# Where the expert-value block stands within a quarter, and the order of the third quarter

## The reference, cut to what matters

```
x = x + 0.5 * ffn(layernorm(x))
x = x + attn(layernorm(x))          # linear attention over states, 16 heads of 8
x = x + 0.5 * ffn(layernorm(x))
```

```
q, k   = x Wq, x Wk                       # 16 heads, 64 wide
w, sel = top2(x Ws);  mix = sigmoid(w) at sel, else 0
v[h]   = sum_e mix[h, e] * (x Wv[e])      # the "values"
attn   = softmax(q k / 8) v               # "scores", "turn", "product"
mask   = top2 of (x Wd) per head
res    = sum_h sum_e mask[h, e] * (attn[h] Wo[e])   # "expand" and "output"
```

## Time and profile before

| | us |
|---|---|
| median of 3 runs | 2470.3 |
| lowest and highest of the 3 | 2469.51 and 2485.37 |
| the profiled execution, its own time | 2470.45 |
| its span, first to last instruction | 2468.7 |
| TensorE busy in it | 2348.8 (95%) |
| ScalarE busy | 2083.6 (84%) |
| VectorE busy | 1960.9 (79%) |
| GpSimd busy | 1136.0 (46%) |
| DMA, mean rate over the span | 157 GB/s |

### The profile page before, as it was taken

The page is one execution under the profiler, slowest core; times in us unless marked ns, Lnnn a source line. Parts: engine busy times, 40 slices in busy tenths (PEclk is TensorE's granted clock), DMA queues, the critical chain, the costliest instruction groups (busy, mean ns, idle before and its releaser), DMA issues.

```text
span 2468.7 us, 119467 instructions
## 1 busy us (share of the span) xinstructions
PE 2348.8 (95%) x49920; PEld 2165.5 (88%) x49920; DVE 1960.9 (79%) x3498; ACT 2083.6 (84%) x6373; POOL 1136.0 (46%) x1126
## 2 busy tenths in 40 slices
PE   3999999999999999999999999999999999999997
PEld 3888898989889898888989889899898989989897
DVE  4887877878888788888888788787887887888874
ACT  3988888888888888888888889888888888889896
POOL 3454544535445355354454444553453544544431
PEclk9999999999999999999999999999999999999999
DMA  4565555655656655566656556566665655565564
GB/s 129 160 162 149 150 158 150 160 152 158 170 150 163 163 157 155 156 162 165 158 157 165 149 156 167 165 163 155 169 159 154 170 157 157 157 167 155 160 173 107
DMA packets 519381, 388.09 MB, mean 157 GB/s; under 512 B 214080, under 2 KB 436160, under 8 KB 510656
## 3 DMA queue, kind: packets, MB, share of 16 engines
q1 hardware_dynamic: 518416, 379.60, 57.5%
q10 hardware_dynamic: 432, 0.85, 0.1%
HBM read 191.64 MB, written 188.74 MB: 154 GB/s over the span
## 4 chain that ended last, share of the span: by engine, by line
PE 82%; DVE 8%; ACT 5%; issue 4%; POOL 1%; DMA 1%; SPq 0%; ACTq 0%; DVEq 0%; POOLq 0%
PE psT L453 18%; PE psS L408 15%; PE psT L470 7%; PE psS L496 6%; PE psT L421 6%; PE psT L472 6%; PE psT L471 6%; PE psT L496 5%; PE psT L465 5%; ACT PB L767 4%; PE psT L435 3%; DVE NMAX L647 1%; DVE QK L706 1%; PE psT L502 1%; DVE ST L729 1%
## 5 line engine op out<-in xcount | busy, mean ns | idle before, releaser
L767 ACT ACTIVATE PB<-psS,NMAX 128x256 f32<-128x256 f32 x2048 | 943.5, 488 | 71.3 <-DVE NMAX L647 68.0
L453 PE MATMUL psT<-V,PT 128*64 128x64 f32 x16384 | 550.0, 224 | 42.9 <-issue 42.2
L453 PEld LDWEIGHTS psT<-V,PT 128*64 128x64 f32 x16384 | 508.7, 138 | 74.0 <-issue 48.8
L706 DVE TENSOR_TENSOR QK<-psT,QK 128x512 fp32r<-128x512 f32 x512 | 341.8, 688 | 205.0 <-ACT QK L776 202.6
L408 PE MATMUL psS<-QK 64*128 64x256 f32 x6144 | 480.4, 291 | 0.2
L767 ACT ACTIVATION_READ_ACCUMULATOR PB<-psS,NMAX 128x1 f32 x2048 | 453.3, 221 | 0.0
L408 PEld LDWEIGHTS psS<-QK 64*128 64x128 f32 x6144 | 404.5, 186 | 32.1 <-issue 29.5
L647 DVE TENSOR_REDUCE NMAX<-psS 128x2 f32<-128x512 f32 x512 | 328.6, 683 | 85.7 <-PE psS L408 84.8
L776 ACT ACTIVATE QK<-psT 128x512 fp32r<-128x512 f32 x512 | 298.1, 621 | 112.5 <-PE psT L472 98.1
L875 POOL TENSOR_TENSOR BT<-MT,diagv 128x1024 f32<-128x1024 f32 x128 | 305.9, 2390 | 136.1 <-DMA MT<-MIXd 136.1
L856 ACT ACTIVATE PT<-psS 128x512 f32<-128x512 f32 x512 | 280.1, 604 | 52.2 <-PE psS L496 48.4
(11 more groups left out here) (119 smaller groups left out, 4589.3 us busy)
## 6 DMA issues: line engine op xcount, KB each, us to landing
Vd<-VM SPq DMA_DIRECT2D x128, 512.0 KB, 3.9
V<-Vd SPq DMA_DIRECT2D x128, 512.0 KB, 5.2
AOd<-AO SPq DMA_DIRECT2D x256, 256.0 KB, 3.8
PJd<-PJ SPq DMA_DIRECT2D x64, 512.0 KB, 2.8
PR<-PJd SPq DMA_DIRECT2D x64, 512.0 KB, 4.0
MIXd<-MIX SPq DMA_DIRECT2D x64, 128.0 KB, 1.7
MT<-MIXd SPq DMA_DIRECT2D x64, 128.0 KB, 4.4
MASKd<-MASKR SPq DMA_DIRECT2D x64, 128.0 KB, 4.0
```

The source lines that it names most:

```text
L453: last = eng.matmul(M[64 * u:64 * u + 64, (t * NT + it) * DH:(t * NT + it + 1) * DH], PT[:, t, jt, cols], V[:, pm % 2, 4 * r + t, jt, :], ...
L706: eng.tensor_tensor(QK[:, 1, ab], bank("qk", m).rearrange("p (k t) -> p k t", k=2), QK[:, 0, ab].bitcast(F32), ALU.subtract).then_inc(free ...
L767: eng.activation(PB[:, ab, j, it, :], psS[:, ab, j, it, :], ACT.Exp, bias=NMAX[:, ab, j, it:it + 1], accum_out=SUM[:, p % 2, it, 4 * r + t ...
```

## The change

The two halves of `values` leave the front of the third and fourth quarters (r = 2 and 3, behind `scores`) and go to the ends of the second and third (r = 1 and 2), right ahead of `turn`. Their places in the ring move with them. On ScalarE `copy_values` stays in r = 2 and r = 3, but now comes ahead of `exponentials(n, 0)`. In the third quarter the q and k projections of the next quarter come right behind `expand`, ahead of `xturn`, `attn_x` and `attn_gram`, on TensorE, in the ring, on VectorE (`QK` ahead of `XT`) and on ScalarE (`rounded` ahead of the copies of `XT`, `AXT` and `GRAM`). No instruction's work is changed; GpSimd's and SyncE's programs are the same.

```diff
--- before.py
+++ after.py
@@ -163,23 +163,19 @@
 
             p, r = divmod(n, 4)
             items = []
-            if r == 2 and runs(p + 1):
-                items += [("values", p + 1, 0, a) for a in range(2)]
-            if r == 3 and runs(p + 1):
-                items += [("values", p + 1, 1, a) for a in range(2)]
             if r == 1 and runs(p - 2):
                 items += [("output", p - 2, i) for i in range(2)]
             if works(n - 1):
                 items.append(("product", n - 1))
             if r == 2 and runs(p - 1):
                 items += [("expand", p - 1, b) for b in range(2)]
+            if works(n + 1):
+                items += [("qk", 2 * n + 2), ("qk", 2 * n + 3)]
             if r == 2:
                 if runs(p + 3):
                     items.append(("xturn", p + 3))
                 if attends(p - 2):
                     items += [("attn_x", p - 2), ("attn_gram", p - 2)]
-            if works(n + 1):
-                items += [("qk", 2 * n + 2), ("qk", 2 * n + 3)]
             if r == 0:
                 if runs(p + 2):
                     items.append(("expert", p + 2, 0))
@@ -199,6 +195,8 @@
                     items.append(("attn_turn", p - 3))
                 if attends(p - 2):
                     items.append(("attn_keys", p - 2))
+            if r in (1, 2) and runs(p + 1):
+                items += [("values", p + 1, r - 1, a) for a in range(2)]
             if works(n):
                 items += [("turn", n, t) for t in (0, 1)]
             return items
@@ -507,10 +505,6 @@
                 if works(n):
                     scores(n, 0)
                     scores(n, 1)
-                if r == 2 and runs(p + 1):
-                    values(p + 1, 0)
-                if r == 3 and runs(p + 1):
-                    values(p + 1, 1)
                 if r == 1 and runs(p - 2):
                     output(p - 2)
                 if works(n - 1):
@@ -518,6 +512,9 @@
                 if r == 2 and runs(p - 1):
                     expand(p - 1, 0)
                     expand(p - 1, 1)
+                if works(n + 1):
+                    project(2 * n + 2)
+                    project(2 * n + 3)
                 if r == 2 and runs(p + 3):
                     q = p + 3
                     wait_vacant(eng, "xturn", q)
@@ -534,9 +531,6 @@
                     for t in range(NT):
                         last = eng.matmul(bank("attn_gram", q)[:, 0:C + 1], AXN[:, t, 0:C], AXN[:, t, :], start=t == 0, stop=t == NT - 1)
                     last.then_inc(full("attn_gram", q))
-                if works(n + 1):
-                    project(2 * n + 2)
-                    project(2 * n + 3)
                 if r in (0, 1) and runs(p + 2):
                     q = p + 2
                     wait_vacant(eng, "expert", q, r)
@@ -591,6 +585,8 @@
                     for k in range(2):
                         last = eng.matmul(M[:, 2 * C + k:2 * C + k + 1], awkv[:, k * C:(k + 1) * C], GRAM[:, C:C + 1], start=True, stop=True)
                     last.then_inc(full("attn_keys", q))
+                if r in (1, 2) and runs(p + 1):
+                    values(p + 1, r - 1)
                 if works(n):
                     turn(n, 1)
                     turn(n, 0)
@@ -695,15 +691,15 @@
                         wait_full(eng, "output", p - 2, 0)
                         wait_full(eng, "output", p - 2, 1)
                         eng.tensor_copy(OT[:, :, 64 * b:64 * b + 64], bank("expand", p - 1, b).rearrange("p (e k) -> p e k", e=E)).then_inc(freed("expand", p - 1, b))
-                if r == 2 and runs(p + 3):
-                    dst = XT[:, (p + 3) % 4]
-                    eng.wait_ge(s_xhi, p + 4)
-                    eng.tensor_tensor(dst[:, 1, :], bank("xturn", p + 3)[:, 0:T], dst[:, 0, :].bitcast(F32), ALU.subtract).then_inc(freed("xturn", p + 3))
                 if works(n + 1):
                     for ab in range(2):
                         m = 2 * n + 2 + ab
                         eng.wait_ge(s_qhi, m + 1)
                         eng.tensor_tensor(QK[:, 1, ab], bank("qk", m).rearrange("p (k t) -> p k t", k=2), QK[:, 0, ab].bitcast(F32), ALU.subtract).then_inc(freed("qk", m))
+                if r == 2 and runs(p + 3):
+                    dst = XT[:, (p + 3) % 4]
+                    eng.wait_ge(s_xhi, p + 4)
+                    eng.tensor_tensor(dst[:, 1, :], bank("xturn", p + 3)[:, 0:T], dst[:, 0, :].bitcast(F32), ALU.subtract).then_inc(freed("xturn", p + 3))
                 if r == 2 and runs(q):
                     equal(1, GM[:, :, :], at + 7)
                 if r == 0 and runs(q):
@@ -790,14 +786,16 @@
                     if q >= 1:
                         eng.wait_ge(s_share, SHARES * (q - 1) + 3)
                     eng.activation(SG[:, :, :], MAXV[:, :, :].rearrange("p k (r g) -> p k g r", g=2)[:, :, 0, :], ACT.Exp, scale=-1.0).then_inc(s_sig)
-                if works(n):
-                    exponentials(n, 0)
                 if r == 2 and runs(p + 1):
                     copy_values(p + 1, 0)
                 if r == 3 and runs(p + 1):
                     copy_values(p + 1, 1)
                 if works(n):
+                    exponentials(n, 0)
+                if works(n):
                     exponentials(n, 1)
+                if works(n + 1):
+                    rounded(n)
                 if r == 2 and runs(p + 3):
                     q = p + 3
                     wait_full(eng, "xturn", q)
@@ -816,8 +814,6 @@
                         wait_full(eng, "attn_keys", attn_pass[nth[q] - 1])
                         wait_freed(eng, "attn_keys", attn_pass[nth[q] - 1])
                     eng.activation(GRAM[:, :], bank("attn_gram", q)[:, 0:C + 1], ACT.Copy).then_inc(freed("attn_gram", q))
-                if works(n + 1):
-                    rounded(n)
                 if r in (0, 1) and runs(p + 2):
                     q = p + 2
                     wait_full(eng, "expert", q, r)
```

## The result

The changed kernel takes **2607.07 us** (median of 4 runs, 2603.05 to 2609.01) against 2473.19 of the kernel before on the same chip: ratio 1.052, interval 1.0484 to 1.0556. The forecast was 2590, slower.

A forecast was written before the change was run, and what follows sets the result against it. The prediction took TensorE to bound the kernel, with almost no slack against ScalarE and VectorE. Waits of 5.6 us per pair of passes, times 32, gave 179, less 57 is +122 on 2470.45: 2590 us, range 2530 to 2630.

The forecast's parts named there:

- Product behind the turns: Third and fourth quarters: `product` waits until ScalarE has copied v0 out of its bank, 0.5 and 0.6 us.
- the rival's aside: At `product`: v0's bank would be free if ScalarE copied v0 ahead of the `PT` copies; rival's chance 5%.
- r = 1: Second quarter: `values` adds 1.1 us, in kind B also waits for the second `qk` bank; +1.1 (A), +1.5 (B).
- r = 2, kind A: Third quarter: `values` waits 1.0 us for banks that VectorE's `QK` and `XT` free; +1.5 us in sum.
- r = 2, kind B: Third quarter: `values` waits for GpSimd's `BT`, ready 9.3 us after `scores`; 11.5 us against 9.57, +1.9.
- r = 3: Fourth quarter: losing `values` gives back nearly nothing, as the turn awaits VectorE's `QK`, which hangs on ScalarE; -0.2 us per kind.
- What comes back: At `product`: all issue stalls, 48.8 us, and 8.5 us of half clock behind them go, together 57 us.
- the stalls stay: Rival: instruction packets arrive late all the same, in other groups than `product`; 2647 us, chance 5%.
- the clock: Rival: the waits for `BT` bring the granted clock down, 1.7 us each; 2644 us, chance 13%.
- faster: Rival: only the instruction starvation moves and the new bank waits are covered; 2413 us, chance 5%.
- no change: Rival: few waits count, none for `BT`, and the fourth quarter gives back what it lost; 2461 to 2490 us, chance 12%.

The follow-up runs named there:

- values_only: The changed kernel with the third quarter put back in the old order (projections last, right ahead of `values`): 2576.94 us, ratio 1.0431 to the kernel before.
- copy_early: The changed kernel with ScalarE copying the values in the quarter in which they are made, ahead of the `PT` copies: 2579.23 us, ratio 1.0452.
- bt_first: The changed kernel with GpSimd making `BT` for the second half of the values ahead of normalising `AAN`: 2580.83 us, ratio 1.0452.
- after_values_wide: The changed kernel with each pair of 64-column matmuls in `values` made one with 128 weight columns: 2696.41 us, ratio 1.0887.
- half0_only: The kernel before with only the first half of the values moved, to the end of the second quarter, its copy ahead of the exponentials: 2491.93 us, ratio 1.0045.
- half1_only: The kernel before with only the second half of the values moved, to the end of the third quarter, its copy ahead of the exponentials: 2540.87 us, ratio 1.0248.

## Why the prediction was right, step by step

- **Product behind the turns:** predicted 0.5 in r = 2 and 0.6 in r = 3; the timeline has 0.40 and 0.41 in r = 2 and 0.54 in r = 3, and there are 112 waits for `VM` in all. Right. But the rival's aside, that copying v0 ahead of the `PT` copies would make it free, is refuted by `copy_early`.
- **r = 1:** predicted +1.1 (A) and +1.5 (B), measured +1.51 and +1.78. Undersized. In kind B the wait is for the predicted bank: `QK` frees it at 1305.25, `values` starts at 1305.35. In kind A the median quarter is 9.98, +1.21, near the prediction. The mean is higher because the turn grew from 1.02 to a mean of 1.32, and that comes from 7 passes in which the turn stops in its middle for a late packet, 6.3 us in all: `values` and the turn are 192 instructions in 2.1 us. The rest of the turn's "issue" entry of 20.9 us stands at the turn's start, most of it in r = 0 and r = 3 of kind A.
- **r = 2, kind A:** from 10.33 (no late packet) to 11.83 predicted; 11.80 in the timeline, 11.67 in the mean. Right, `XT`'s bank as foreseen (with part of the wait already at `attn_gram`, for `QK`), and `values_only` took the wait away.
- **r = 2, kind B:** 11.5 predicted; 11.64 in the timeline, 11.71 in the mean. `BT` at 9.27 against 9.3, since VectorE began `NMAX` 1.00 after `scores` instead of 1.53. Right, shown by `bt_first`. The terms written there (9.3 + 1.1 + 1.0) make 11.4; what they leave out is that `values` starts 0.26 after `BT` is ready.
- **r = 3:** 9.0 predicted in both kinds; 8.96 and 8.98. Right, and the cause, ScalarE, shown by `copy_early`.
- **What comes back:** predicted 57, and this is the term that was mis-sized. The late packets fell from 42.9 us to 12.7, so 30.2 came back, and up to 8.5 with the half clock of five stretches: about 39. Of the 18.6 that are missing, 5.9 are the reading at the weight loads (48.8 for 42.9) and 12.7 are packets that still come late, in the turn and in `scores`. That share of the rival "the stalls stay" came true. With 39 back, the 135 us mean that the waits and moves cost 174 us, 5.4 per pair against 5.6 predicted. So the sum of the waits was 5 us too high and the return 18 too high, and the difference of the two is the distance between +122 and 135. Single quarters were off by more, r = 1 and r = 2 of kind B upward and r = 2 of kind A downward, and partly cancelled; that much is luck.
- **The rival "the clock":** no in this kernel, but closer than it looks. Its 26 waits of about 1.4 us for `BT` brought no fall of the granted clock:

```profile
200.00:2400.00 2200.00, 2024.46 (x42986) 1854.18 (x42985) 1695.82 (x3036) 1772.00 (x5491) 992.82 (x986) 1.00 0.56 150
```

  In `after_values_wide` TensorE has the same 26 waits, of 1.4 to 2.1 us, and 17 of them were followed by 3.4 us at half the clock, as in the line below, where `values` took 2.48 us instead of 2.00. What makes the difference no run shows.

```profile
1371.93 2.48 PE L418 MATMUL psT<-PR,BT 64*128 64x64 f32 x32 [1.41 <-POOL BT L870]
```

- **The rivals "faster" and "no change":** `half0_only` came nearest to what they needed, and still r = 1 paid 1.6 to 1.7 for 1.1 us of matmuls.

The rule of the Trainium skill weighed in the prediction (Runtime: NRT & Kernel Launch, "Instruction fetch mechanics"), that fetching is hidden behind dispatch, does not hold where a block of 256 instructions is used up in 3.1 us. The stalls of 42.9 us stand at one place of the block, and `values_half_instr`, with half the instructions in `values`, is 2.4% faster without them.

## What to carry to other kernels

With a ring of PSUM banks, write out the ring after a move and ask of every neighbour when it is read out: each mover of a step also changes who waits for whom four places later, and a step that waits for nothing of its own may be what hid a wait. Taking work out of a stretch that another engine bounds gives back only the slack, while putting it elsewhere is paid in full. And a matmul stream of many small tiles can be bound by instruction supply; here halving the instructions was worth more than any order tried, but only in the form in which the bigger tile was not slower. To tell such a stall from a wait for a bank, look whether it lies in the middle of a group and always at the same place of a block of 256 instructions.

## What was not expected of the hardware

- Late instruction packets move with the instruction density: 42.9 us in the kernel before, most of it in `product` behind `values`, 12.7 after the change, 1.1 with half the instructions in `values`. They also move into groups that were not touched: 19.9 us in `scores` of `half1_only`.
- All 276 such stalls in fourteen traces stand at number 193 to 195 of a block of 256 instructions.
- Two fp32 matmuls with 64 weight columns side by side are much faster than one with 128: `values` 150.3 against 249.6 us busy, `product` 550.0 against 970.4.
- A transpose of the same shape (64 rows, 128 columns, 64 streamed) takes 1.02 us for 32, the matmul 1.85.
- The same wait of 1.4 us brought the clock down in 0 of 26 cases in one kernel, and waits of 1.4 to 2.1 us at the same place did in 17 of 26 in another.
